# Delta-rule attention turns: each triangular system as two diagonal blocks of 64 and a corner

## The chip, the cores and the metric

The kernel runs on one core of one Trainium2 chip. The core has a matrix engine (PE, with its weight loads listed apart as PEld), a vector engine (DVE), a scalar engine (ACT), a general engine that here mostly issues indirect DMAs (POOL) and a queue for plain DMAs (SP). The metric is device time in microseconds (us) of one execution. Three runs of the kernel before took 1979.56 to 1985.12 us, median 1981.37 us.

## The reference, cut to what matters

Four stages run one after the other on a sequence of 4096 tokens of width 256: a delta-rule attention, a mixture of experts (8 experts, top 2), an RWKV layer and a ternary feed-forward net. The change touches the first only. Its recurrence, cut to the two memories `fH` (fast) and `sH` (slow), is

```
def step(carry, inp):
    pred = (q_t @ fH + q_t @ sH) * 0.5
    d_fast = outer(k_t, v_t) - outer(k_t, k_t @ fH)
    fH = fast_alpha * fH + (1 - fast_alpha) * d_fast
    d_slow = outer(k_t, v_t) - outer(k_t, k_t @ sH)
    sH = slow_alpha * sH + (1 - slow_alpha) * (i_t > 0.5) * d_slow
    ...
    o = p_t[0] * (q_t @ fH) + p_t[1] * (q_t @ sH) + p_t[2] * ns
```

Over a chunk of 128 tokens the steps of one memory are a unit lower triangular system of 128 unknowns, (I + L) Y = X, where L is strictly lower triangular (gram matrix of the keys times decays) and X holds 128 columns: 64 for the values, 64 for the keys.

## The kernel before, in words

The 4096 tokens are 32 chunks of 128. A *turn* (16 of them, `TURNS`) takes two chunks, `j` = 0 and 1, and each chunk has two memories, `m` = 0 and 1, so a turn solves four systems. While the systems of turn t are solved, the same turn carries the *tail* of turn t-1 (state update and outputs, which go from chunk to chunk), the *head* of turn t+1 (transposes, grams, masks, right sides) and, from turn 2 on, one piece per turn of the later work on blocks of 512 tokens (neuron state, output projection, norm, router logits, ranks, places). The pieces for odd turns differ from those for even ones.

Before the change a system is solved by doubling on the right side: Y = (I - L)(I + L^2)(I + L^4)... X, in 8 levels (`LEVELS`), the first 5 of which (`SQUARES`) also square the matrix. `L` holds each matrix and its transpose (128x128 each), because a matmul needs its left operand transposed.

* PE, `level` (L1216): at level n, for each chunk, up to four 128x128 squares into banks 0 and 1 (L1229, L1230), then the product with the two right sides into banks 2 and 3 (L1238). Every fp32 matmul is two PE instructions in the trace.
* ACT, `square` (L968): copies the four squares of a chunk, 128x512, from PSUM to the other buffer of `L` (L972; the last level only the transposes, L975).
* DVE, `apply` (L579): adds the product to the right side `X`, 128x256 a chunk (L588), 16 times a turn. From level 5 on the sums go into `Z` (partial_sums), since no further square is taken: levels 5 to 7 apply the same matrix three times. `masks` (L567) makes `L` from the gram in PSUM: two 128x256 products a chunk (L574) and one for `QM` (L577).

In the trace `X` is part of the tile `st`, and all banks are called `bank`.

Each engine works through a list written out by hand in `turn(u)`, one for PE (L1338), DVE (L751), ACT (L1041) and POOL (L382); semaphores count levels (`sq_ps`, `sq_cp`, `ap_ps`, `ap_rdy`). Nothing is reordered: an engine that waits at level n holds back all that stands behind it in its list. POOL's list also paces the loads of the weight check (`load_words`, L374, which waits for `fold_words` on DVE, L637), adds the hidden weight blocks by DMA in turns 12 to 15 (`hidden_sums`, L399) and scatters the normed tokens to the experts (`scatter`, L345), eight indirect DMAs for each block of 512 tokens. The expert stage starts by gathering from what was scattered (`xg`, L1521), when the last scatter has landed.

Of the kernel before, what the change touches and what calls it, by code (L numbers as in the profile page):

```python
# [25 lines left out]
SQUARES = 5  # L26
# [50 lines left out]
def build(nc, A):  # L77
# [5 lines left out]
    with ctx:  # L83
# [109 lines left out]
        QM = sb("QM", [128, 2, 2, 2, 128], to=pa)  # L193
        YT = sb("YT", [128, 2, 128], to=pa)
# [224 lines left out]
        def _(dve):  # L419
# [146 lines left out]
            dve.sem_inc(pp_rdy, 1)  # L566

            def masks(t, p, j, bk=4):
# [11 lines left out]
            def apply(t, p, n):  # L580
                for j in range(2):

                    dve.wait_ge(ap_ps, t * (2 * LEVELS) + (2 * n + j + 1))
                    if n == 0:
                        dve.wait_ge(x_rdy, t * 2 + (j + 1))
                    x_ = X[:, p, j, :, :, :].rearrange("p a m d -> p (a m d)")
                    z_ = Z[:, j, :, :, :].rearrange("p a m d -> p (a m d)")
                    V.tensor_tensor(z_ if SQUARES <= n < LEVELS - 1 else x_, x_, B[2 + j][:, 0:256],  # L588
                                    ALU.subtract if n == 0 else ALU.add).then_inc(ap_rdy, 1)
# [298 lines left out]
        def _(act):  # L888
# [78 lines left out]
            def square(t, p, n):  # L967
                for j in range(2):  # L968
                    act.wait_ge(sq_ps, t * (2 * SQUARES) + (2 * n + j + 1))
                    src = B[j][:, :].rearrange("p (a n) -> p a n", a=4)  # L970
                    if n < SQUARES - 1:
                        A_.activation(L[:, p, j, (n + 1) % 2, :, :], src, ACT.Copy).then_inc(sq_cp, 1)  # L972
                    else:

                        A_.activation(L[:, p, j, (n + 1) % 2, 1::2, :], src[:, 1::2, :], ACT.Copy).then_inc(sq_cp, 1)  # L975
# [57 lines left out]
            def turn(u):  # L1033
# [34 lines left out]
                at(u, 1, 5, columns, 0)  # L1068
                if head:
# [65 lines left out]
        def _(pe):  # L1135
# [81 lines left out]
            def level(t, p, n, first):  # L1217
                for j in range(2):
                    if n == 0:
                        pe.wait_ge(l_rdy, t * 2 + (j + 1))  # L1220
                        pe.wait_ge(x_rdy, t * 2 + (j + 1))
                    elif n <= SQUARES:
                        pe.wait_ge(sq_cp, t * (2 * SQUARES) + (2 * (n - 1) + j + 1))
                    Ln = L[:, p, j, min(n, SQUARES) % 2, :, :]
                    if n < SQUARES:
                        for m in range(2):
                            a, b_ = Ln[:, 2 * m, :], Ln[:, 2 * m + 1, :]
# [4 lines left out]
                    if n > 0:  # L1232
                        pe.wait_ge(ap_rdy, t * (2 * LEVELS) + (2 * (n - 1) + j + 1))
                    elif not first:
                        pe.wait_ge(ap_rdy, t * (2 * LEVELS) + (j - 1))
                    for m in range(2):
                        right = X[:, p, j, :, m, :] if n <= SQUARES else Z[:, j, :, m, :]
                        last = T.matmul(B[2 + j][:, 0:256].rearrange("p (a m d) -> p a m d", a=2, m=2)[:, :, m, :],  # L1238
                                        Ln[:, 2 * m + 1, :], right, start=True, stop=True)
# [98 lines left out]
            def turn(u):  # L1338

                t, p, deltas, head, tail = u, u % 2, u < TURNS, u + 1 < TURNS, 1 <= u <= TURNS  # L1340
                for n in range(LEVELS):
                    if deltas:
                        level(t, p, n, not tail)
# [2163 lines left out]
```

## Time and profile before

| what | value |
|---|---|
| median of 3 runs | 1981.37 us |
| the profiled execution | 1982.84 us |
| its span, first to last instruction | 1981.0 us |
| PE busy over the span | 1830.8 us (92%) |
| DVE busy | 1468.3 us (74%) |
| ACT busy | 1113.4 us (56%) |
| POOL busy | 307.7 us (16%) |
| the turns | about 89 to 461 us |
| first matmul of the expert stage | 525.3 us |

Busy time is the time in which at least one instruction of an engine runs. A row of the view by windows gives, for a stretch of the span, the busy time of each engine with its number of instructions, the TensorE clock granted (1.00 is full), the share of the DMA engines and what they moved. A turn is taken here from the first transposes of its tail (L1246) to those of the next. In rows of groups, of lines and of the timeline an arrow `out<-in` names the tiles, and brackets give the idle time ahead of an instruction and what ended it. A PE row says which part of the array the matmul uses, rows by columns: `64*128` is a contraction over 64 partitions.

### The profile page before, as it was taken

Reading aid. Unit: us, or ns where it says so; the run is one execution under the profiler, and the core shown is the slowest. Engines: PE = TensorE matmul, PEld = TensorE weight load, DVE = VectorE, ACT = ScalarE, POOL = GpSimd, SP = SyncE. Lnnn points to the kernel's source line nnn. Section 1 sums busy time; section 2 is a strip of 40 time slices with the busy share of each in tenths; the row PEclk is TensorE's granted clock in tenths of the full one; section 3 lists DMA queues with packets and bytes.
Section 4 is the critical chain, followed back from the end, with each engine's and each line's share of the span. In section 5 each row is a group of like instructions: output and inputs, shape, how many; then the busy total and the mean of one; then the engine's idle time right before and its main releaser. Section 6 shows DMA issues by size and latency. Waiting matters only on the chain. (4 is left out here: it accounts for less than half of the span.)

```text
span 1981.0 us, 31299 instructions
## 1 busy us (share of the span) xinstructions
PE 1830.8 (92%) x10880; PEld 1564.9 (79%) x10880; DVE 1468.3 (74%) x2959; ACT 1113.4 (56%) x1997; POOL 307.7 (16%) x282
## 2 busy tenths in 40 slices
PE   7999999997399999999687969999999999999999
PEld 5688888886399999999465647776788888888887
DVE  7567888887477766767689988787776776776675
ACT  3656666664244444343599876664565465466454
POOL 0000002235433223233101011111000000000000
PEclk9999999996699999999799979999999999999999
DMA  3099543359435334322444572333333243142241
GB/s 112 29 378 407 180 161 124 103 117 223 148 65 120 86 86 96 64 44 39 117 106 88 126 210 87 149 117 118 117 139 128 67 167 128 64 170 106 65 170 65
DMA packets 107985, 251.78 MB, mean 127 GB/s; under 512 B 8992, under 2 KB 51616, under 8 KB 99616
## 3 DMA queue, kind: packets, MB, share of 16 engines
q1 hardware_dynamic: 82288, 201.16, 28.6%
q0 software_dynamic: 23680, 46.28, 12.8%
q10 hardware_dynamic: 1888, 2.67, 0.4%
q8 instruction: 75, 1.23, 0.2%
q14 instruction: 54, 0.44, 0.1%
HBM read 172.88 MB, written 107.61 MB: 142 GB/s over the span
## 5 line engine op out<-in xcount | busy, mean ns | idle before, releaser
L1566 POOL DMA_INDIRECT tokens_behind_spare_rows<-yg,row_of_token x70 | 120.2, 1717 | 300.1 <-DVE row_of_token L1729 272.4
L1661 ACT ACTIVATE h<-bank,b1s 128x256 f32<-128x256 f32 x280 | 125.3, 472 | 37.7 <-PE bank L1489 23.4
L1650 ACT ACTIVATE yg<-yt,own_gates 128x256 f32<-128x256 f32 x68 | 31.0, 502 | 191.1 <-DVE yt L1724 184.7
L3244 ACT ACTIVATE hidden_quarter<-hidden_quarter,scl 128x512 f32<-128x512 f32 x96 | 67.6, 721 | 118.9 <-DVE hidden_quarter L3080 118.3
L1238 PE MATMUL bank<-st,L 128*128 128x128 f32 x768 | 117.1, 279 | 13.3 <-DVE st L588 13.2
L972 ACT ACTIVATE L<-bank 128x512 f32<-128x512 f32 x128 | 75.1, 593 | 93.8 <-PE bank L1230 93.5
L2465 PE MATMUL bank<-split_0h,hidden_weights 128*128 128x512 f32 x320 | 126.5, 395 | 0.0
L2465 PE MATMUL bank<-split_1h,hidden_weights 128*128 128x512 f32 x320 | 125.4, 392 | 0.1
L2466 PE MATMUL bank<-split_0l,hidden_weights 128*128 128x512 f32 x320 | 125.3, 391 | 0.0
L2466 PE MATMUL bank<-split_1l,hidden_weights 128*128 128x512 f32 x320 | 125.3, 391 | 0.0
L1230 PE MATMUL bank<-L 128*128 128x128 f32 x640 | 119.0, 276 | 0.0
L1238 PEld LDWEIGHTS bank<-st,L 128*128 128x128 f32 x768 | 100.4, 193 | 17.8 <-DVE st L588 7.0
L588 DVE TENSOR_TENSOR st<-st,bank 128x256 f32<-128x256 f32 x192 | 75.1, 417 | 52.3 <-PE bank L1238 51.5
L1229 PE MATMUL bank<-L 128*128 128x128 f32 x512 | 100.9, 279 | 0.7
L2465 PE MATMUL bank<-split_2h,hidden_weights 128*128 128x512 f32 x256 | 101.4, 396 | 0.0
L1758 DVE TENSOR_TENSOR hsl<-h,hsh 128x512 fp32r<-128x512 f32 x140 | 96.9, 692 | 4.8
L2466 PE MATMUL bank<-split_2l,hidden_weights 128*128 128x512 f32 x256 | 100.2, 391 | 0.0
L1230 PEld LDWEIGHTS bank<-L 128*128 128x128 f32 x640 | 95.1, 193 | 0.0
L3032 DVE SCALAR_TENSOR_TENSOR hidden_quarter<-bank,scl,x_tok 128x512 f32<-128x512 f32 x64 | 47.4, 747 | 55.7 <-ACT x_tok L3207 55.7
L3039 DVE TENSOR_TENSOR split_2l<-hidden_quarter,split_2h 128x1024 fp32r<-128x1024 f32 x48 | 59.1, 1251 | 35.4 <-ACT split_2h L3226 35.4
L1229 PEld LDWEIGHTS bank<-L 128*128 128x128 f32 x512 | 78.8, 193 | 7.2 <-issue 2.7
L1712 DVE COPY raw_gates<-xg 128x8 f32<-128x8 f32 x36 | 8.0, 223 | 102.0 <-PE bank L1594 101.3
(493 smaller groups left out, 6088.3 us busy)
## 6 DMA issues: line engine op xcount, KB each, us to landing
hidden_weights<-hidden_weight_blocks SPq DMA_DIRECT2D x64, 1024.0 KB, 4.8
z_by_expert<-zero SPq DMA_DIRECT2D x64, 520.0 KB, 15.9
hidden_weight_blocks<-in_ffn_dram SPq DMA_DIRECT2D x14, 1024.0 KB, 13.2
ckb<-in_ffn_dram POOLq DMA_DIRECT2D x32, 352.0 KB, 5.5
xg<-z_by_expert SPq DMA_DIRECT2D x36, 260.0 KB, 3.4
x_tok<-in_w_dram SPq DMA_DIRECT2D x8, 1024.0 KB, 7.9
x_tok<-x_T SPq DMA_DIRECT2D x16, 512.0 KB, 6.0
x_tok<-after_time_mix SPq DMA_DIRECT2D x15, 512.0 KB, 8.2
```

What stands on the lines that cost most here:

```text
L588: V.tensor_tensor(z_ if SQUARES <= n < LEVELS - 1 else x_, x_, B[2 + j][:, 0:256], ALU.subtract if n == 0 else ALU.add).then_inc(ap_rdy, 1)
L972: A_.activation(L[:, p, j, (n + 1) % 2, :, :], src, ACT.Copy).then_inc(sq_cp, 1)
L1229: T.matmul(B[j][:, 256 * m:256 * m + 128], b_, a, start=True, stop=True)
L1230: last = T.matmul(B[j][:, 256 * m + 128:256 * m + 256], a, b_, start=True, stop=True)
L1238: last = T.matmul(B[2 + j][:, 0:256].rearrange("p (a m d) -> p a m d", a=2, m=2)[:, :, m, :], Ln[:, 2 * m + 1, :], right, start=True, stop ...
L1566: pool.indirect_dma_start(x2_d, bass.IndirectOffsetOnAxis(to_row[:, j:j + 1].bitcast(u32), 0), yg[:, j, :], None, compute_op=ALU.add).then ...
L1661: nc.scalar.activation(h32[:, m, :], B[m % 4][:, 0:TT], ACT.Gelu_apprx_tanh, bias=b1s[:, e * KH + m:e * KH + m + 1]).then_inc(h_act, 1)
L1758: V.tensor_tensor(hs[1][:, m:m + 2, :], h32[:, m:m + 2, :], f32(hs[0][:, m:m + 2, :]), ALU.subtract).then_inc(h_rdy, 1)
L2465: nc.tensor.matmul(out, w, x[0], start=first, stop=False, **more)
L2466: return nc.tensor.matmul(out, w, x[1], start=False, stop=last, **more)
L3039: V.tensor_tensor(lo[:, ks, :], QB[source_of(use)][:, ks, :], f32(hi[:, ks, :]), ALU.subtract).then_inc(ring_rdy, 1)
L3244: A_.activation(QB[to][:, m, :], src, ACT.Gelu, scale=scl[:, off[lay.name] + row:off[lay.name] + row + 1]).then_inc(g_act, 1)
```

## The change

Each 128x128 system is cut into two diagonal blocks of 64 and the corner below: with L = [[A, 0], [C, B]], the solution is Y1 = (I+A)^-1 X1 and Y2 = (I+B)^-1 (X2 - C Y1). Block A lies on partitions 0 to 63 and block B on partitions 64 to 127 of the same columns (`half`), so that one instruction of DVE or ACT handles both, and PE gets two matmuls, one for each half.

* The inverse is doubled in place of the right side: `apply` 0 sets it to I minus the block (transposed), levels 1 to 5 add the product with the next square, 128x128 a chunk. `twin` is a pair of identities of 64 in what was part of `Z`.
* Squares are 64x64 (two halves, two memories, matrix and transpose), and `square` copies 128x256 a chunk, in the last level 128x128. The copy of square 1 also waits for `apply` 0 of its chunk.
* Level 6 multiplies the corner by the inverse of B (only rows 64 to 127 of the array, output on partitions 0 to 63) and then both inverses by the right sides; `apply` 6 is a copy of 128x256. Level 7 takes the corner's part off on partitions 64 to 127.
* ACT gets `corner_products` (L995), two copies of 64x128, between the columns of the router input and the two `right_side` calls of the next turn. It waits for level 6 on PE.
* `masks` makes the two blocks with two products of 64 partitions and the corner with a third.

A turn has 128 matmuls for its systems where it had 68. Of the 128, 112 have a moving side of 64 columns and 16 one of 128; all stand in blocks of 64x64 of the array.

```diff
-                for m in range(2):
-                    gm = B[bk][:, m * 128:(m + 1) * 128].rearrange("p (o n) -> p o n", o=1)
-                    V.tensor_tensor(L[:, p, j, 0, 2 * m:2 * m + 2, :], gm.broadcast_to([128, 2, 128]),
-                                    maskL[:, m, :, :], ALU.mult)
+                gram = B[bk][:, 0:256].rearrange("p (m o n) -> p m o n", m=2, o=1)
+                for h in range(2):
+                    V.tensor_tensor(pair(p, j, 0)[half[h]], gram[half[h], :, :, half[h]].broadcast_to([DS, 2, 2, DS]),
+                                    maskL[half[h], :, :, half[h]], ALU.mult)
+                V.tensor_tensor(corner(p, j)[half[1]], gram[half[1], :, 0, half[0]], maskL[half[1], :, 0, half[0]], ALU.mult)
...
             def apply(t, p, n):
                 for j in range(2):
-                    dve.wait_ge(ap_ps, t * (2 * LEVELS) + (2 * n + j + 1))
...
-                    V.tensor_tensor(z_ if SQUARES <= n < LEVELS - 1 else x_, x_, B[2 + j][:, 0:256],
-                                    ALU.subtract if n == 0 else ALU.add).then_inc(ap_rdy, 1)
+                    if n == 0:
+                        dve.wait_ge(l_rdy, t * 2 + (j + 1))
+                        V.tensor_tensor(inv, twin, pair(p, j, 0)[:, :, 1, :], ALU.subtract).then_inc(ap_rdy, 1)
+                        continue
+                    dve.wait_ge(ap_ps, t * (2 * (LEVELS - 1)) + (2 * (n - 1) + j + 1))
+                    if n <= SQUARES:
+                        V.tensor_tensor(inv, inv, B[2 + j][:, 0:128].rearrange("p (m n) -> p m n", m=2),
+                                        ALU.add).then_inc(ap_rdy, 1)
+                    elif n < LEVELS - 1:
+                        V.tensor_copy(x_, B[2 + j][:, 0:256]).then_inc(ap_rdy, 1)
+                    else:
+                        V.tensor_tensor(x_[half[1]], x_[half[1]], B[2 + j][half[1], 0:256], ALU.subtract).then_inc(ap_rdy, 1)
...
             def square(t, p, n):
                 for j in range(2):
+                    if n == 1:
+                        act.wait_ge(ap_rdy, t * (2 * LEVELS) + (j + 1))
+                    src = B[j][:, 0:256].rearrange("p (m f n) -> p m f n", m=2, f=2)
...
+            def corner_products(t, p):
+                for j in range(2):
+                    act.wait_ge(sq_ps, t * (2 * SQUARES + 2) + (2 * SQUARES + j + 1))
+                    A_.activation(corner_inverse(p, j)[half[0]], B[j][half[0], 0:128].rearrange("p (m n) -> p m n", m=2),
+                                  ACT.Copy).then_inc(sq_cp, 1)
...
                 at(u, 1, 5, columns, 0)
+                if deltas:
+                    corner_products(t, p)
                 if head:
                     right_side(t + 1, 1 - p, 0)
...
                             if n < SQUARES - 1:
-                                T.matmul(B[j][:, 256 * m:256 * m + 128], b_, a, start=True, stop=True)
-                            last = T.matmul(B[j][:, 256 * m + 128:256 * m + 256], a, b_, start=True, stop=True)
+                                for h in half:
+                                    T.matmul(B[j][h, 128 * m + 64:128 * m + 128], ab[h, m, 0, :], ab[h, m, 1, :], start=True, stop=True)
+                            for h in half:
+                                last = T.matmul(B[j][h, 128 * m:128 * m + 64], ab[h, m, 1, :], ab[h, m, 0, :], start=True, stop=True)
...
+                    if n <= SQUARES:
+                        for m in range(2):
+                            for h in half:
+                                last = T.matmul(B[2 + j][h, 64 * m:64 * m + 64], ab[h, m, 0, :], inv[h, m, :], start=True, stop=True)
+                    elif n < LEVELS - 1:
+                        for m in range(2):
+                            last = T.matmul(B[j][half[0], 64 * m:64 * m + 64], corner(p, j)[half[1], m, :], inv[half[1], m, :],
+                                            start=True, stop=True)
+                        last.then_inc(sq_ps, 1)
+                        pe.wait_ge(x_rdy, t * 2 + (j + 1))
+                        for m in range(2):
+                            for h in half:
+                                last = T.matmul(out[h, :, m, :], inv[h, m, :], X[h, p, j, :, m, :], start=True, stop=True)
+                    else:
+                        for m in range(2):
+                            last = T.matmul(out[half[1], :, m, :], corner_inverse(p, j)[half[0], m, :], X[half[0], p, j, :, m, :],
+                                            start=True, stop=True)
                     last.then_inc(ap_ps, 1)
```

On PE, at level 1 of an odd turn, this is what stands for one chunk and the tail's first matmul behind the second, before the change (L1229 and L1230 are the squares, L1238 the products with the right sides; one row is one matmul unless it says x2):

```order
L1229 MATMUL bank<-L 128x128 [waits square_taken]
L1230 MATMUL bank<-L 128x128
L1229 MATMUL bank<-L 128x128
L1230 MATMUL bank<-L 128x128
L1238 MATMUL bank<-st,L 128x2x64 [waits X_ready]
L1238 MATMUL bank<-st,L 128x2x64
L1256 MATMUL bank<-state,YT 128x128 [waits pred_taken,state_ready,YT_ready]
```

and this is what stands there now (L1257 and L1259 squares, L1267 products with the inverse, each row pair once for the lower and once for the upper half):

```order
L1257 MATMUL bank<-L 64x64 [waits square_taken]
L1257 MATMUL bank<-L 64x64
L1259 MATMUL bank<-L 64x64 x2
L1257 MATMUL bank<-L 64x64 x2
L1259 MATMUL bank<-L 64x64 x2
L1267 MATMUL bank<-L 64x64 [waits X_ready]
L1267 MATMUL bank<-L 64x64 x3
L1297 MATMUL bank<-state,YT 128x128 [waits pred_taken,state_ready,YT_ready]
```

The six matmuls of a chunk became twelve of a quarter of the array each, and the waits stand where they stood.

On ACT, behind the last squares of an odd turn, this stood before the change (L975 the last square, L963 to L965 the head's transposed keys, L1026 the router columns, from L952 on the right sides of the next turn):

```order
L975 ACTIVATE L<-bank 128x2x128 [waits square_in_psum] x2
L963 ACTIVATE st<-bank 128x2x128 [waits decayed_q_ready,kqT_in_psum]
L964 ACTIVATE gram_right_sides<-bank 64x2x128
L965 ACTIVATE gram_right_sides<-bank 64x128
L1026 ACTIVATE zT<-bank 128x512 [waits z1T_in_psum]
L952 ACTIVATE KR<-st,rev 128x64 [waits kq_ready,pred_in_psum]
```

and this stands there now (L993 the last square, L998 the corner products):

```order
L993 ACTIVATE L<-bank 128x2x64 [waits square_in_psum] x2
L979 ACTIVATE st<-bank 128x2x128 [waits decayed_q_ready,kqT_in_psum]
L980 ACTIVATE gram_right_sides<-bank 64x2x128
L981 ACTIVATE gram_right_sides<-bank 64x128
L1050 ACTIVATE zT<-bank 128x512 [waits z1T_in_psum]
L998 ACTIVATE L<-bank 64x128 [waits square_in_psum] x2
L968 ACTIVATE KR<-st,rev 128x64 [waits kq_ready,pred_in_psum]
```

ACT has a new wait, for level 6 of the same turn on PE, ahead of the right sides and all that stands behind them.

## Rows read from the trace of the kernel before

**Rows 1.** Windows, turns 0, 1, 3, 9, 10: us, busy (x) by engine, PEclk, DMA

```profile
89.10:116.67 27.57, 24.13 (x179) 21.98 (x179) 18.88 (x60) 18.62 (x52) 2.15 (x4) 0.94 0.71 260
116.67:136.49 19.82, 19.60 (x168) 18.86 (x167) 13.07 (x41) 12.08 (x36) 1.04 (x2) 1.00 1.03 407
156.31:178.73 22.42, 21.20 (x177) 19.69 (x176) 16.73 (x51) 14.69 (x44) 2.07 (x4) 1.00 1.03 407
295.85:319.70 23.85, 22.64 (x188) 21.03 (x187) 20.08 (x70) 18.80 (x52) 6.03 (x8) 1.00 0.58 188
319.70:343.53 23.83, 22.83 (x195) 21.45 (x194) 18.93 (x68) 12.48 (x36) 6.72 (x8) 1.00 0.24 75
```

**Rows 2.** Lines by form, PE, turns 9 and 10 (295.85 to 343.53 us)

```profile
L1238 PE MATMUL bank<-st,L 128*128 128x128 f32 x98 | 14.9, 278 | 1.6 <-DVE st L588 1.6
L1230 PE MATMUL bank<-L 128*128 128x128 f32 x80 | 14.8, 275 | 0.0
```

**Rows 3.** Waits, turns 9 and 10: total us, times, longest us

```profile
ACT L L972 <- PE bank L1230: 11.6, 10, 3.5
DVE st L588 <- PE bank L1238: 4.8, 5, 1.5
```

**Rows 4.** Timeline, PE, one level of turn 9: start, us, form, count

```profile
307.38 0.39 PE L1230 MATMUL bank<-L 128*128 128x128 f32 x2
...
307.60 0.61 PE L1238 MATMUL bank<-st,L 128*128 128x128 f32 x4
...
308.05 0.61 PE L1230 MATMUL bank<-L 128*128 128x128 f32 x4
```

**Rows 5.** Timeline, PE, matmuls over 64 partitions and their neighbours

```profile
88.09 1.12 PE L1200 MATMUL bank<-vgT,small_weights 64*128 64x512 f32 x2
...
185.86 0.81 PE L1214 MATMUL bank<-gram_right_sides,st 128*128 128x384 f32 x2
186.60 1.14 PE L1308 MATMUL bank<-woN,big 64*128 64x256 f32 x8
187.67 0.49 PE L1229 MATMUL bank<-L 128*128 128x128 f32 x2
```

**Rows 6.** Lines L1160 and L1200: weight loads of 64 and 128 columns, ns min/median/max

```profile
L1160 PEld LDWEIGHTS bank<-hT,small_weights x16: 132/134/136, 26.3 to 95.0; 128*64 128x64 f32 x16
...
L1200 PEld LDWEIGHTS bank<-vgT,small_weights x16: 182/184/186, 23.5 to 88.2; 64*128 64x128 f32 x16
```

**Rows 7.** Lines by form, DVE, turns 9 and 10

```profile
L588 DVE TENSOR_TENSOR st<-st,bank 128x256 f32<-128x256 f32 x24 | 9.2, 416 | 4.9 <-PE bank L1238 4.8
...
L574 DVE TENSOR_TENSOR L<-bank,maskL 128x256 f32<-128x256 f32 x8 | 3.0, 417 | 0.4 <-PE bank L1214 0.4
...
L595 DVE TENSOR_TENSOR Wb<-st,bank 128x128 f32<-128x128 f32 x4 | 1.1, 280 | 0.0
```

**Rows 8.** Lines by form, ACT, turns 9 and 10

```profile
L972 ACT ACTIVATE L<-bank 128x512 f32<-128x512 f32 x16 | 9.4, 593 | 11.6 <-PE bank L1230 11.6
...
L975 ACT ACTIVATE L<-bank 128x256 f32<-128x256 f32 x4 | 1.3, 373 | 0.0
```

**Rows 9.** Timeline behind turn 14: POOL's last check load and scatters, DVE's last places

```profile
439.51 0.58 POOL L374 DMA_DIRECT2D ckb<-in_ffn_dram  x1 [12.15 <-DVE lowb L637]
...
477.48 1.04 POOL L345 DMA_INDIRECT z_by_expert<-Z,slotz  x1 [0.30 <-issue]
...
503.17 0.17 DVE L748 CAST slotz<-SF 128x8 int32<-128x8 f32 x1
...
518.58 0.97 POOL L345 DMA_INDIRECT z_by_expert<-Z,slotz  x1 [0.30 <-issue]
```

**Rows 10.** Windows and PE timeline where the clock fell, turn 0

```profile
109.90:112.90 3.00, 0.20 (x2) 0.00 (x1) 2.69 (x17) 1.54 (x5) 0.00 (x0) 1.00 1.01 408
113.00:116.00 3.00, 2.63 (x12) 2.63 (x13) 1.97 (x4) 0.00 (x0) 1.02 (x2) 0.50 1.03 413
...
114.39 0.64 PE L1229 MATMUL bank<-L 128*128 128x128 f32 x2
```

More of the change, by code:

```diff
@@ L193, in build @@
         QM = sb("QM", [128, 2, 2, 2, 128], to=pa)
+        Lp = L[:, :, :, :, :, :].rearrange("p b j s a n -> p b j s (a n)")
+        pair = lambda p, j, s_: Lp[:, p, j, s_, 0:256].rearrange("p (m f n) -> p m f n", m=2, f=2)
+        inverse = lambda p, j: Lp[:, p, j, 0, 256:384].rearrange("p (m n) -> p m n", m=2)
+        corner = lambda p, j: Lp[:, p, j, 0, 384:512].rearrange("p (m n) -> p m n", m=2)
+        corner_inverse = lambda p, j: Lp[:, p, j, 1, 256:384].rearrange("p (m n) -> p m n", m=2)
+        twin = Z[:, 1, 0, :, :]
         YT = sb("YT", [128, 2, 128], to=pa)
@@ L566, in _ @@
             dve.sem_inc(pp_rdy, 1)
+            for h in range(2):
+                for m in range(2):
+                    go(V.tensor_copy(twin[half[h], m, :], ident[half[h], half[h]]))
             def masks(t, p, j, bk=4):
@@ L1215, in grams, with level @@
                          start=True, stop=True).then_inc(g_ps, 1)
-            def level(t, p, n, first):
+            def level(t, p, n):
                 for j in range(2):
@@ L1225, in level @@
+                    ab, inv = pair(p, j, n % 2), inverse(p, j)
+                    out = B[2 + j][:, 0:256].rearrange("p (a m d) -> p a m d", a=2, m=2)
                     if n < SQUARES:
                         for m in range(2):
-                            a, b_ = Ln[:, 2 * m, :], Ln[:, 2 * m + 1, :]
                             if n < SQUARES - 1:
-                                T.matmul(B[j][:, 256 * m:256 * m + 128], b_, a, start=True, stop=True)
-                            last = T.matmul(B[j][:, 256 * m + 128:256 * m + 256], a, b_, start=True, stop=True)
+                                for h in half:
+                                    T.matmul(B[j][h, 128 * m + 64:128 * m + 128], ab[h, m, 0, :], ab[h, m, 1, :], start=True, stop=True)
+                            for h in half:
+                                last = T.matmul(B[j][h, 128 * m:128 * m + 64], ab[h, m, 1, :], ab[h, m, 0, :], start=True, stop=True)
@@ L1231, in level @@
                         last.then_inc(sq_ps, 1)
[L1232 to L1239, printed above, removed]
+                    if n == 0:
+                        continue
@@ new lines, in level @@
+                    pe.wait_ge(ap_rdy, t * (2 * LEVELS) + (2 * (n - 1) + j + 1))
+                    if n <= SQUARES:
[12 more added lines that the diff above has]
+                    else:
+                        for m in range(2):
+                            last = T.matmul(out[half[1], :, m, :], corner_inverse(p, j)[half[0], m, :], X[half[0], p, j, :, m, :],
+                                            start=True, stop=True)
@@ L1342, in turn @@
                     if deltas:
-                        level(t, p, n, not tail)
+                        level(t, p, n)
                     if tail:
```

20 lines of the change are left out of this document (10 added, 10 removed).

## The prediction

> **What bounds the kernel now.** I first cut the attention stage into turns with the view by windows. From turn 5 to turn 14 a turn lasts 23.85 us, and PE is busy for 22.64 to 22.83 us of it at full clock; DVE is busy for 20.08 us in an odd turn and 18.93 us in an even one, ACT for 18.80 and 12.48 us [rows 1]. Turns 1 and 2 last 19.82 us each with PE at 19.60, turns 3 and 4 some 22.4 us with PE at 21.2, turn 0 27.57 us with PE at 24.13 [rows 1]. So PE is the bound of every turn. The view of waits says the same from the other side: in two turns ACT waits 11.6 us for squares and DVE 4.8 us for products [rows 3]. The lines by form name what fills PE: the squares and the products of the four systems [rows 2], 68 matmuls or 136 instructions a turn.
>
> A saving in the turns must also get through to the end. The timeline behind the turns shows that the expert stage waits for POOL's scatters, not for DVE: the last places are made at 503.17 us, but the last scatter is issued at 518.58 us [rows 9]. POOL's list runs from its last check load at 439.51 us (released by DVE at the end of turn 14) through hidden sums to 32 scatters in one row from 477.48 us on [rows 9]. This chain of some 80 us hangs on the end of turn 14 alone. What turns 0 to 14 save is passed on in full; what turn 15 saves is not, as long as DVE's end stays ahead of POOL's (15.4 us of slack).
>
> **PE's share of the change.** A matmul of 128 columns costs two instructions at 0.112 us: four of L1238 fill the 0.45 us from 307.60 to 308.05 [rows 4]. So the systems now take 136 x 0.112 = 15.2 us a turn, and all else on PE 22.7 - 15.2 = 7.5 us.
>
> The trace has no matmul in a 64x64 block, so its price must be bounded. *Length:* a weight load of 64 columns is 50 ns shorter than one of 128 (134 against 184) [rows 6], and 0.112 less 0.050 is 0.06; half of 0.112 is 0.056. I take 0.058 us an instruction with 64 columns. From above the bound is the full 0.112. *Side by side:* L1308 is four matmuls over 64 partitions, two on the lower half and then two on the upper. Its eight instructions of 256 columns start at 186.60 and are followed at 187.67 [rows 5]. One after the other they would need 8 x 2 x 0.112 = 1.79 us; they took 1.07. A single one over 64 partitions gains nothing: L1200, two instructions of 512 columns, takes 1.12 us, 2 x 4 x 0.112 and its tail [rows 5]. So the two halves ran beside each other, even with the second half two matmuls further down the list. The new code puts the halves next to each other.
>
> The sum a turn, in pairs: 36 pairs of squares and 20 pairs of products, two instructions each at 0.058, make 6.5 us; 4 corner matmuls alone 0.46; 4 pairs of 128 columns at 0.112 make 0.9 and the 4 single ones of level 7 another 0.9. Together 8.8 us. If the halves take turns it is 72 + 40 matmuls at 2 x 0.058 = 13.0, plus 0.46 + 1.8 + 0.9: 16.1 us.
>
> Going in and out of the half-array work costs something: behind L1308 the next pair takes 0.49 us where an undisturbed one takes 0.39 [rows 4, 5], and L1308's 1.07 us are 0.17 over four paired steps of 2 x 0.112. I charge 0.25 us a round trip (0 to 0.3) and count seven a turn, one for each level that has full-array work behind it: 1.75 us. The Trainium skill ("TensorEngine Tiling (Array Packing)", Key Properties) says that a change of tiling mode drains TensorE; the 0.10 us behind L1308 agrees with that, and without the drains the sum would be 1.75 us a turn shorter on PE. PE then needs 7.5 + 8.8 + 1.75 = 18 us of a steady turn, and is no longer the bound.
>
> **What is late next.** DVE. A 128x128 product with PSUM takes 0.280 us, a 128x256 one 0.416 [rows 7]; 12 of the 16 `apply` steps shrink that way, 12 x 0.136 = 1.6 us. The copy of level 6 and the 64-partition step of level 7 keep 256 columns and are charged as before, since an instruction's length follows its columns. The two L574 of a chunk stay at 256 columns, and the corner adds one of 128: 2 x 0.2 = 0.4 us back. Net 1.2 us, so DVE needs 18.9 us in an odd turn and 17.7 in an even one, 18.3 on average. It now waits 23.84 - 19.5 = 4.3 us a turn. If all waiting went, a turn would be 18.3 us; if none went, 22.6. Most of it is for products and squares on PE [rows 3], which come in half the time, but not all can go: after each `apply` DVE needs a matmul, the drain of that matmul and a semaphore back before the next one, and in some levels it has little else to do meanwhile. In odd turns it also waits for ACT.
>
> ACT saves 8 copies from 0.593 to 0.373 us [rows 8], 1.8 us, and pays two corner copies of half a L975's columns, estimated at 0.25: in odd turns 18.8 - 1.3 = 17.5 us. It gets a new wait: behind `corner_products` stand the right sides, the last columns, `prepare`, and then square 0 of the next turn: work that used to fill ACT's idle time behind the squares and now starts only at level 6. With 17.5 us of its own and a wait in the middle, ACT is the second bound of odd turns. I put two thirds of DVE's old waiting on top of its work: 18.3 + 2.9 = 21.2 us.
>
> **The sum.** Turns 5 to 14: 10 x (23.84 - 21.2) = 26.4 us. Turns 1 and 2 have DVE at 13.1 us and PE then at 15: I take 16.5, halfway between PE's work and the old length, 2 x 3.3 = 6.6. Turns 3 and 4: PE 21.2 - 15.2 + 10.5 = 16.5; I take 19.2, 2 x 3.2 = 6.4. Turn 0: PE falls by 4.7 us, but it already waits for DVE at the end [rows 10], so 3.5. Together 43 us. The profiled execution took 1982.84 us (span 1981.0 and 1.84 around it), 1.5 us over the median of the runs, less than they differ by; 1982.8 - 43 = 1940 us.
>
> **Rivals.**
> *A, the forecast*, 1940 us; with turns of 20.2 to 22.6 us its own range is 1915 to 1965.
>
> *B, waits nearly vanish.* If DVE becomes full, a steady turn is 19 us and saves 4.85, the early ones 4 to 5: 10 x 4.85 + 5 x 4.2 = 70, so 1913 us. For it: PE would have 18 us of work and ACT 17.5. Against: three lists in fixed order, each near full, wait for each other.
>
> *C, the halves take turns: slower.* In the 64x64 blocks both halves write the same PSUM bank, while L1308 wrote one bank with each half, so the row does not show this case. PE would need 7.5 + 16.1 + 1.75 = 25.4 us, with its 1 us of waits 26.4, 2.5 over now: 15 x 2.5 = 38, so 2020 us (1997 without the drains). It decides from the point where the systems cost more than 23.85 - 7.5 - 1.75 - 1 = 13.6 us on PE, which is when less than about a third of the 7.3 us between both sums is gained by overlap. For it speaks a rule of the Trainium skill ("TensorEngine Tiling (Array Packing)", Gotcha 1: PSUM Pressure): different row tiles cannot use one PSUM bank at the same time. No run so far shows that. Against: the halves end on different partitions, which L1308's did not. If each small instruction kept 0.112 us and no pair overlapped, it would be 256 x 0.112 = 28.7 us, 13.5 over now, 2185 us; the shorter weight load [rows 6] speaks against that.
>
> *D, the clock falls: slower or nothing.* Before it fell to half at 112.9 us PE had run 0.20 us of 3.0, and at half clock a pair of squares took 0.64 us instead of 0.39 [rows 4, 10]. After the change PE has more gaps. If half of PE's 18 us of work were done at the lower clock, they would be 27, and a turn at least as long: 15 x 3 = 45 over now, 2028 us. Against: that fall came when PE had next to nothing for 3 us at a stretch, while the 3.2 us that a turn would leave it are spread over eight levels.
>
> *E, nothing passes.* DVE keeps all its waits and ACT's new one adds to them: a steady turn of 23.5 and early ones 0.5 shorter, 6 us, 1977 us.
>
> **Chances.** A 0.58, B 0.13, C 0.13, D 0.08, E 0.08. A measurement of this kernel tells about 0.3%, 6 us, from no change. A and B are faster; of E and D a little falls on that side too: faster 0.74. Within 0.3%: half of E and a part of C without drains, 0.08. Slower: 0.18. The range is 1908 to 2000 us: it leaves out the better half of B and most of C and D, nearly 0.2 in all.
>
> **What would show it.** Right: MATMUL rows of the new square lines in pairs with an interval of some 0.06 us, steady turns near 21 us, DVE at 18 to 19 us of each, PE at 1.00, the scatters unchanged in number and still the last to end before the expert stage, which starts some 43 us earlier; from there on all as before. Wrong in the price: rows of the two halves one after the other (C), or a PEclk below 1.00 in the turns (D). Wrong in what is late next: DVE idle as long as before and ACT standing at the corner products, or places on DVE later than the scatters. A change behind 530 us other than the shift would speak against the whole account.

## The result: 1966.0 us, a third of the forecast saving

The changed kernel takes 1965.99 us (median of 6 runs, 1962.74 to 1973.05) beside 1980.46 us of the kernel before (6 runs, 1977.98 to 1985.12). The ratio is 0.9925, with a 95% interval of 0.991 to 0.9941: faster by 0.75%, about 15 us, where 43 were forecast. The profiled execution of after took 1962.74 us with a span of 1961.0.

**The turns after the change.** The view by windows, cut at the first matmul of L1287 (the y transposes, which open a tail), for turns 3, 6, 7, 8, 10, 12 and 14. Columns: the stretch; its length and PE's busy time with its count; then PEld, DVE, ACT, POOL; the granted clock, DMA share, GB/s.

```profile
148.06:172.21 24.15, 21.11 (x294) 17.01 (x295) 16.79 (x53) 13.42 (x48) 2.06 (x4) 0.75 1.03 406
...
214.07:235.44 21.37, 17.98 (x313) 14.79 (x313) 18.80 (x71) 11.61 (x41) 2.06 (x4) 1.00 0.58 197
235.44:257.21 21.77, 17.62 (x306) 14.37 (x307) 19.28 (x71) 16.21 (x51) 2.05 (x4) 1.00 0.68 233
257.21:281.10 23.89, 20.80 (x312) 17.43 (x313) 19.05 (x71) 11.71 (x41) 2.05 (x4) 0.86 0.30 92
...
303.07:326.90 23.83, 20.81 (x313) 16.91 (x313) 18.73 (x71) 11.60 (x41) 6.41 (x8) 0.86 0.25 77
...
349.71:375.19 25.48, 22.38 (x312) 18.45 (x313) 18.67 (x71) 11.72 (x41) 6.44 (x8) 0.80 0.30 93
...
396.80:421.99 25.19, 22.41 (x312) 18.35 (x313) 18.30 (x71) 11.61 (x41) 10.86 (x12) 0.80 0.72 156
```

Read the clock beside the length. Turns 6 and 7, at 1.00, last 21.37 and 21.77 us with PE at 18.0 and 17.6: forecast were 21.2 and 18. The turns at 0.86 last 23.8 to 23.9, as long as any turn before [rows 1]; at 0.80 they last 25.2 to 25.5, longer than before. Before, every turn from 1 on was at 1.00 ([rows 1] has turns 1, 3, 9 and 10).

**The price of the new matmuls.** The timeline of PE in a level of turn 6 (start, us, form, count), the answer to [rows 4]:

```profile
217.46 0.28 PE L1257 MATMUL bank<-L 64*64 64x64 f32 x4
217.58 0.28 PE L1259 MATMUL bank<-L 64*64 64x64 f32 x4
217.70 0.28 PE L1257 MATMUL bank<-L 64*64 64x64 f32 x4
217.81 0.28 PE L1259 MATMUL bank<-L 64*64 64x64 f32 x4
217.93 0.40 PE L1267 MATMUL bank<-L 64*64 64x64 f32 x8
218.26 0.49 PE L1297 MATMUL bank<-state,YT 128*128 128x128 f32 x2
218.68 0.33 PE L1257 MATMUL bank<-L 64*64 64x64 f32 x4
```

Each group of four instructions is two matmuls, one on each half, into one bank. The next group starts 0.117 us later: two steps of 0.058 us. One after the other, four would take 0.23. The last two rows show the way out of the half-array work and back: the eight L1267 fill 0.23 us by that step, and L1297 starts 0.10 us after that; it needs 0.22 us, and the next L1257 starts 0.20 us after that. (A turn's systems have 116 matmuls with 64 columns and 12 with 128, not 112 and 16: the four corner matmuls, L1270, have 64.)

**What PE did before the clock fell.** Its timeline at level 5 of turn 10, and then the windows ahead of the fall and in it:

```profile
314.50 0.49 PE L1297 MATMUL bank<-state,YT 128*128 128x128 f32 x2
315.53 0.41 PE L1235 MATMUL bank<-ident,st 128*128 128x128 f32 x2 [0.54 <-DVE QM L587]
317.03 1.12 PE L1267 MATMUL bank<-L 64*64 64x64 f32 x16 [1.09 <-DVE L L600]
```

```profile
315.00:317.00 2.00, 0.41 (x2) 0.20 (x3) 1.97 (x8) 1.62 (x7) 0.00 (x0) 0.99 0.00 0
317.00:323.80 6.80, 6.77 (x51) 5.05 (x52) 3.00 (x11) 2.75 (x12) 0.00 (x0) 0.50 0.25 80
```

PE waits 0.54 us, works 0.41, waits 1.09. From 317.0 on it is granted 0.50, its lower level of 1.2 GHz, for 6.8 us, in which it is busy without a break while DVE works 3.00 us. But the same waits stand at level 5 of turn 6, which has 1.00 from end to end:

```profile
227.04 0.41 PE L1235 MATMUL bank<-ident,st 128*128 128x128 f32 x2 [0.54 <-DVE QM L587]
228.54 0.65 PE L1267 MATMUL bank<-L 64*64 64x64 f32 x15 [1.08 <-DVE L L600]
```

And before the change a wait of 1.00 us on DVE (L588) stood in each even turn from 4 to 14, with no fall. So a fall follows some of these waits and not others; what decides is not shown by any run here. Nine of the turns 2 to 14 of after show a clock under 1.00, with no wait in these turns over 1.14 us (the fall of turn 1 follows one of 3.5 us at the end of turn 0); over turns 1 to 14 the clock is 0.90, where before had 1.00.

The waits of turn 10 are for DVE, whose list ahead of them reads:

```profile
313.89 0.85 DVE L583 TENSOR_TENSOR L<-bank,maskL 64x256 f32<-64x256 f32 x2
314.66 0.29 DVE L585 TENSOR_TENSOR L<-bank,maskL 64x128 f32<-64x128 f32 x1
314.96 0.42 DVE L587 TENSOR_TENSOR QM<-bank,maskQ 128x256 f32<-128x256 f32 x1
...
315.81 0.87 DVE L696 SCALAR_TENSOR_TENSOR x_tok<-bank,small,x_tok 128x256 f32<-128x256 f32 x2
316.60 0.48 DVE L600 TENSOR_TENSOR L<-L,bank 128x128 f32<-128x128 f32 x2
```

The masks and a residual (L696) stand between PE's products and the L600 that takes them. Another wait of 0.98 us stands at the start of most turns, for L632.

**DVE and ACT.** Lines by form in turns 6 and 7 (an even and an odd one), the two L596 of turn 6 and of turn 7 from the timeline, and a wait, the answers to [rows 7], [rows 8] and [rows 3]:

```profile
L600 DVE TENSOR_TENSOR L<-L,bank 128x128 f32<-128x128 f32 x20 | 5.0, 282 | 1.5 <-PE bank L1267 1.4
L583 DVE TENSOR_TENSOR L<-bank,maskL 64x256 f32<-64x256 f32 x8 | 3.4, 420 | 0.9 <-PE bank L1240 0.8
...
L596 DVE TENSOR_TENSOR L<-partial_sums,L 128x128 f32<-128x128 f32 x4 | 1.5, 425 | 0.0
...
L585 DVE TENSOR_TENSOR L<-bank,maskL 64x128 f32<-64x128 f32 x4 | 1.1, 286 | 0.0
...
L991 ACT ACTIVATE L<-bank 128x256 f32<-128x256 f32 x16 | 5.8, 376 | 7.7 <-PE bank L1259 7.7
```

```profile
215.68 1.06 DVE L596 TENSOR_TENSOR L<-partial_sums,L 128x128 f32<-128x128 f32 x2
238.97 0.49 DVE L596 TENSOR_TENSOR L<-partial_sums,L 128x128 f32<-128x128 f32 x2
```

```profile
ACT L L998 <- PE bank L1270: 4.8, 2, 2.5
```

The mean of 425 ns for L596 is a mixture: 0.28 us each in turn 7, as long as L600, and 0.56 to 0.57 in turn 6. Over the whole trace its median is 284 ns; it is long in turns 3, 4, 6 and 8 alone.

**Behind the turns.** POOL's last check load, its last scatter, DVE's last places and the expert stage's first matmul, the answer to [rows 9]:

```profile
423.45 0.58 POOL L380 DMA_DIRECT2D ckb<-in_ffn_dram  x1 [13.06 <-DVE lowb L653]
...
501.35 0.97 POOL L351 DMA_INDIRECT z_by_expert<-Z,slotz  x1 [0.30 <-issue]
...
487.09 0.17 DVE L764 CAST slotz<-SF 128x8 int32<-128x8 f32 x1
...
508.32 1.12 PE L1635 MATMUL bank<-ident,xg 128*128 128x128 f32 x4 [21.46 <-DMA xg<-z_by_expert]
```

Turn 14 ends 16.9 us earlier (421.99 for 438.88), the last scatter 17.2 and the expert stage's first matmul 17.0 (525.34 before). The chain on POOL carried the saving through unchanged.

### The profile page after: what moved, and what is told of

Its sections match the earlier page's. It is cut to its first block and busy times, and to the rows that moved or that the text cites. A ratio compares the mean times of both kernels' runs of the same rounds, so it can differ in the third digit from the quotient of the medians.

```text
span 1961.0 us, 35208 instructions
## 1 busy us (share of the span) xinstructions
PE 1775.7 (91%) x12800; PEld 1478.8 (75%) x12800; DVE 1459.8 (74%) x2995; ACT 1086.2 (55%) x2029; POOL 306.9 (16%) x282
## 5 line engine op out<-in xcount | busy, mean ns | idle before, releaser
L1259 PE MATMUL bank<-L 64*64 64x64 f32 x1280 | 87.0, 232 | 0.2 <-issue 0.2
L991 ACT ACTIVATE L<-bank 128x256 f32<-128x256 f32 x128 | 46.5, 377 | 70.0 <-PE bank L1259 69.0
L1257 PE MATMUL bank<-L 64*64 64x64 f32 x1024 | 78.0, 243 | 5.8 <-DVE QM L587 5.6
L1528 PE MATMUL bank<-xTh,w_1h 128*128 128x256 f32 x288 | 80.8, 281 | 2.7 <-ACT h L1702 2.7
L1528 PE MATMUL bank<-w_1h,hsh 128*128 128x256 f32 x288 | 82.1, 285 | 0.6 <-DVE yt L1765 0.6
L1529 PE MATMUL bank<-w_1l,hsh 128*128 128x256 f32 x288 | 80.3, 279 | 0.0
L1530 PE MATMUL bank<-w_1h,hsl 128*128 128x256 f32 x288 | 80.3, 279 | 0.0
L1529 PE MATMUL bank<-xTl,w_1h 128*128 128x256 f32 x288 | 80.2, 278 | 0.0
```

The source lines that it names most:

```text
L1257: T.matmul(B[j][h, 128 * m + 64:128 * m + 128], ab[h, m, 0, :], ab[h, m, 1, :], start=True, stop=True)
L1259: last = T.matmul(B[j][h, 128 * m:128 * m + 64], ab[h, m, 1, :], ab[h, m, 0, :], start=True, stop=True)
L1528: nc.tensor.matmul(out, a[0], b[0], start=first, stop=False)
L1529: nc.tensor.matmul(out, a[0], b[1], start=False, stop=False)
L1530: return nc.tensor.matmul(out, a[1], b[0], start=False, stop=last)
```

## The experiments

T1: falls of TensorE's clock inside the turns ate most of the missing gain. T2: ACT's new wait at the corner products sets the turn. T3: DVE's list sets it. Every kernel was timed beside the kernel before on its chip; ratios are to that kernel. The first four ran together (before: 1983.05 us), the next four (1981.61), then the last three (1982.86).

| run | us | ratio (95%) |
|---|---|---|
| after | 1965.99 | 0.9925 (0.991 to 0.9941) |
| e1_fill | 1949.61 | 0.9833 (0.982 to 0.9845) |
| e1_fill_short | 1977.06 | 0.9965 (0.9946 to 0.9983) |
| e2_corner_dve | 1966.28 | 0.9909 (0.9895 to 0.9924) |
| e3_order | 1954.60 | 0.9859 (0.9842 to 0.9875) |
| e4_both | 1943.09 | 0.9803 (0.9786 to 0.9821) |
| e5_mask_twice | 1957.51 | 0.9883 (0.9866 to 0.99) |
| e6_diag | 1946.75 | 0.9818 (0.9804 to 0.9833) |
| e7_diag_order | 1938.06 | 0.9767 (0.9753 to 0.9782) |
| e8_half_fill | 1934.51 | 0.976 (0.9747 to 0.9774) |
| e9_corner_full | 1942.49 | 0.9793 (0.978 to 0.9807) |
| e10_no_start | 1943.24 | 0.9808 (0.9789 to 0.9827) |

**Work for PE's waits** (e1_fill; e1_fill_short has 1 column in the place of 256):

```diff
+            def fill(k, bk=3):
+                for _ in range(k):
+                    T.matmul(B[bk][:, 256:256 + 256], I_, filler[:, 0:256], start=True, stop=True)
...
+                            pe.wait_ge(ap_rdy, t * (2 * LEVELS))
+                            fill(2)
                             y_transposes(t - 1, 1 - p)
...
+                            if n == 0 and tail and u % 2 == 1:
+                                fill(1)
                             transposes(t + 1, 1 - p, n // 4)
...
                         at(u, 1, 3, neuron_back)
+                        if tail and u % 2 == 0:
+                            pe.wait_ge(sq_cp, t * (2 * SQUARES + 2) + 2 * SQUARES)
+                            fill(2, 1)
```

> Adds to TensorE, in every turn after the first, two matmuls of 256 columns that nobody reads (some 0.45 us each) while it waits at the start of the turn, one more ahead of the keys' transposes in odd turns, and two behind level 4 in even turns. T1 (falls of TensorE's clock inside the turns ate the missing gain): PEclk stays at or near 1.00 from turn 1 to turn 14, even turns come down from 23.8-25.5 to 21.5-22.5 us, and the time to 1946-1956 us, 10 to 20 us under the changed kernel's 1966. T2 (ScalarE's new wait at the corner products sets the turn): the clock may rise, but turns keep their length; 1964-1970 us. T3 (VectorE is the bound, because the masks on partition halves cost more than forecast): the same as T2, with VectorE over 95% busy in the turns that were at full clock already.

> The same added matmuls at the same places with the same waits, but of one column instead of 256. All theories: the time of the changed kernel, 1963-1970 us, with the same falls of the clock to half in the turns. T1 stands only if this one does not gain while the long ones do; if both gain, it is the added waits and not the clock.

Turns 9 and 10 with the long fillers, then two turns with the short ones, by windows:

```profile
278.28:299.89 21.61, 19.00 (x313) 15.41 (x313) 19.11 (x71) 16.20 (x51) 6.02 (x8) 1.00 0.61 206
299.89:320.76 20.87, 19.59 (x322) 16.15 (x321) 18.72 (x71) 11.61 (x40) 6.41 (x8) 1.00 0.27 87
```

```profile
288.23:312.11 23.88, 20.76 (x313) 17.47 (x313) 19.29 (x71) 16.20 (x51) 6.03 (x8) 0.86 0.50 164
312.11:336.02 23.91, 21.85 (x320) 18.38 (x321) 18.81 (x71) 11.70 (x41) 6.42 (x8) 0.86 0.23 76
```

PE was given work that nobody reads, and the even turn became 3 us shorter: 20.87 for 23.83. The clock stays at 1.00 from turn 4 to turn 14; the waits for DVE that are left there are 0.9 us at most. That the filler works through the clock alone is seen in turn 6, which is at 1.00 in all three kernels: it lasts 21.37 us in after and 21.36 with either filler. The ratio falls by 0.0092, 18 us, as T1 said. The same places and waits with one column gain nothing; they lose 8 us (1977 where 1963 to 1970 were expected), because now nearly every turn has a fall. That the control is slower than after, and not equal, was in no theory; why the falls come more often there is left open. The difference between the two kernels, 27 us, is that between filler of 256 columns and of 1.

**ACT's wait taken away** (e2_corner_dve): the corner copies move into DVE's level 6.

```diff
-            def corner_products(t, p):
...
                     elif n < LEVELS - 1:
+                        V.tensor_copy(corner_inverse(p, j)[half[0]],
+                                      B[j][half[0], 0:128].rearrange("p (m n) -> p m n", m=2)).then_inc(sq_cp, 1)
                         V.tensor_copy(x_, B[2 + j][:, 0:256]).then_inc(ap_rdy, 1)
```

> The two copies of the corner products go from ScalarE to VectorE (in the list just ahead of the level 6 copy), so ScalarE no longer waits there. T2 (that wait sets the turn): ScalarE's 6.7 us of waiting in turns 9 and 10 go, the right sides and the preparation of the next turn come up to 3.9 us earlier, odd turns shrink by 1 to 3 us; 1942-1955 us. T1 and T3: VectorE gets two copies of 128 columns a turn, about 0.25 us each, on its own path: turns 0 to 0.5 us longer, 1966-1974 us.

The time is that of after. Turns 6 and 7, at full clock as in after, keep their length to 0.05 us:

```profile
214.00:235.37 21.37, 17.86 (x313) 14.80 (x313) 19.09 (x73) 9.93 (x32) 2.06 (x4) 1.00 0.57 193
235.37:257.19 21.82, 17.70 (x306) 14.49 (x307) 19.65 (x73) 17.69 (x54) 2.05 (x4) 1.00 0.68 230
```

In turn 7 ACT no longer waits at that place and DVE works 0.4 us more (19.65 for 19.28), and the turn is as long as it was: ACT's wait is slack, and T2 falls.

**DVE's list in another order** (e3_order): no operation more or less.

```diff
-                at(u, 0, 4, residual, 0)
                 at(u, 1, 3, neurons)
...
                     rows_w(t - 1, 1 - p, 1)
+                at(u, 0, 4, residual, 0)
                 at(u, 0, 4, residual, 1)
...
+                if tail and head:
+                    partial_outputs(t - 1, 1)
                 if head:
                     masks(t + 1, 1 - p, 1)
...
                 if tail and head:
-                    partial_outputs(t - 1, 1)
                     rest_of_outputs(t - 1, 1)
```

> Only VectorE's list is put in another order: the residual of the even turns goes from ahead of level 4's subtraction to behind the last rows of the turn, and the second partial output from behind the masks of the second chunk to ahead of them. T1: TensorE's waits of about 1 us ahead of level 5 and at the turn's start shrink to under 0.5 us, most of the falls of the clock at these two places go, even turns come down by 1 to 3 us; 1945-1960 us. T2: nothing, 1963-1969 us. T3: VectorE has the same work and no fewer microseconds, 1963-1969 us.

The wait of 1.09 us ahead of level 5 became 0.30, and the even turn without a fall is the shortest of all; the turn after it still has one:

```profile
310.48 0.68 PE L1268 MATMUL bank<-L 64*64 64x64 f32 x16 [0.30 <-DVE L L600]
```

```profile
296.71:317.15 20.44, 17.96 (x312) 14.70 (x312) 18.82 (x71) 12.78 (x45) 6.43 (x8) 1.00 0.29 89
317.15:339.67 22.52, 19.10 (x306) 15.72 (x307) 19.29 (x71) 15.04 (x47) 6.05 (x8) 0.92 0.19 58
```

Within T1's interval (1945 to 1960), and it needs no filler: the place of DVE's side work in its list had opened this wait. It is not the cause of all falls. Nine of the turns 2 to 14 still show a lower clock; over turns 1 to 14 it is 0.93, between 0.90 in after and 0.99 with the long fillers. And a part of the gain is not the clock: at 1.00 in both kernels, turn 6 lasts 21.02 us for 21.37 and turn 13 21.24 for 21.61.

**Both together** (e4_both): e1_fill and e3_order, and

```diff
+                            if u == 1:
+                                pe.wait_ge(pp_rdy, 1)
+                                fill(7, 6)
...
+                        if tail and deltas and u % 2 == 1:
+                            pe.wait_ge(sq_cp, t * (2 * SQUARES + 2) + 2 * SQUARES)
+                            fill(2, 1)
                         at(u, 1, 3, neuron_back)
```

> The long fillers of the first experiment, VectorE's list in the order of the fourth, and fillers at the three places where a fall was left: seven ahead of the wait of 3.5 us at the end of turn 0, and two ahead of the neurons' back transposes in odd turns. T1 (the clock): turns 1 and 3 lose another 1 to 1.7 us, every turn from 1 to 14 is at 1.00; with the clock full, the order itself is worth little, since VectorE has the same work: 1943-1950 us beside 1950 for the fillers alone. If the order also shortens waits by itself (the chain through VectorE sets the turn at full clock): 1935-1943 us. If the fillers now stand where TensorE does not wait and delay it: 1950-1957 us.

1943.1 us, where T1's interval ends and that of the shorter chain begins, so the time alone does not choose. All turns from 1 to 14 are at 1.00, turn 3 lasts 19.75 us in place of 24.15; the steady ones 20.9 to 21.4. At full clock the order, with two more fillers in odd turns, is worth 0.4 us in these (21.23 for 21.61) and next to nothing in even ones.

**What sets the turn at full clock?** Four kernels. e5_mask_twice adds to e1_fill one mask operation a chunk; e6_diag changes e1_fill so that one mask operation does for two, at the price of more matmuls. The edit of e5, then that of e6 on DVE and on PE:

```diff
+                V.tensor_tensor(corner(p, j)[half[0]], gram[half[0], :, 0, half[1]], maskL[half[0], :, 0, half[1]], ALU.mult)
```

```diff
-                gram = B[bk][:, 0:256].rearrange("p (m o n) -> p m o n", m=2, o=1)
-                for h in range(2):
-                    V.tensor_tensor(pair(p, j, 0)[half[h]], gram[half[h], :, :, half[h]].broadcast_to([DS, 2, 2, DS]),
-                                    maskL[half[h], :, :, half[h]], ALU.mult)
...
+                gram = B[bk][:, 0:256].rearrange("p (a m o n) -> p a m o n", a=2, m=2, o=1)
+                V.tensor_tensor(pair(p, j, 0), gram[:, 0].broadcast_to([128, 2, 2, DS]), maskL[:, :, :, half[0]], ALU.mult)
...
-                T.matmul(B[bk][:, 0:384], KQT[:, p, j, 0, :], GR[:, j, :, :].rearrange("p a n -> p (a n)"),
+                for h in half:
+                    T.matmul(B[bk][h, 0:128], KQT[:, p, j, 0, h], GR[:, j, 0:2, h], start=True, stop=True)
+                T.matmul(B[bk][half[1], 128:256], KQT[:, p, j, 0, half[1]], GR[:, j, 0:2, half[0]], start=True, stop=True)
+                T.matmul(B[bk][:, 256:384], KQT[:, p, j, 0, :], GR[:, j, 2, :], start=True, stop=True).then_inc(g_ps, 1)
```

> The kernel with the long fillers, and a second mask operation of the corner's size for each chunk (on the other half of the partitions; nothing reads it), 0.29 us twice a turn on VectorE. T3 at full clock (VectorE's list sets the turn once the clock is kept): turns 0.4 to 0.6 us longer, 15 turns, 1955.5-1959 us beside the fillers' 1950. If VectorE's waits absorb it: 1949-1952 us.

> The kernel with the long fillers, with TensorE writing the two diagonal blocks of each Gram matrix side by side (four matmuls in the place of one, the same 384 columns), so that one mask operation of 128x256 takes the place of the two on partition halves: VectorE 0.42 us less a chunk, 0.84 us a turn. If VectorE's list sets the turn at full clock: 0.5 to 0.9 us a turn less, 1936-1942 us. If it does not: 1948-1952 us.

Turns 9 and 10 of e5_mask_twice, then of e6_diag, to be read against the 21.61 and 20.87 us of e1_fill:

```profile
279.42:301.56 22.14, 19.01 (x313) 15.42 (x313) 19.58 (x73) 16.41 (x52) 6.04 (x8) 1.00 0.61 202
301.56:322.75 21.19, 19.45 (x321) 16.13 (x321) 19.04 (x73) 11.53 (x39) 6.42 (x8) 1.00 0.27 86
```

```profile
274.37:295.84 21.47, 19.31 (x326) 16.14 (x325) 18.45 (x69) 16.05 (x51) 6.03 (x8) 1.00 0.63 209
295.84:316.85 21.01, 20.37 (x333) 17.01 (x332) 18.05 (x69) 11.70 (x41) 6.42 (x8) 1.00 0.29 87
```

With 0.79 us more on DVE the two turns are 0.85 longer. (The 1957.5 us of e5 lie in the interval for DVE's list, but its profiled execution also has a fall, in turn 11, which lasts 24.76 us; the turns at 1.00 are the evidence.) With 1.33 us less on DVE and 1.09 more on PE the two turns are the same, 42.48 us. The 1946.75 us of e6 lie in neither interval, 1936 to 1942 nor 1948 to 1952: DVE's work counts where it is added, but taking it away at PE's expense gives nothing in these turns.

e7_diag_order joins e4_both and e6_diag; e8_half_fill is e7 with `256:256 + 128` and `filler[:, 0:128]`; e9_corner_full is e7 with the edit of e2; e10_no_start is e7 with `fill(2 if u == 1 else 0)` at the turn's start.

> Everything of the other three together: long fillers at all places, VectorE's new order, diagonal Gram blocks with one mask operation. If VectorE's list sets the turn: the gains add up, 1928-1940 us. If not: 1943-1950 us, as the fillers with the new order.

> The fastest version so far (fillers at all places, VectorE's new order, diagonal Gram blocks; 1938 us) with fillers of 128 columns in the place of 256, so TensorE has about 0.9 us a turn less to do. If TensorE, at 20 of 21 us with the fillers, now sets the turn: 0.3 to 0.9 us a turn less, 1925-1934 us. If the chain from engine to engine sets it: 1936-1940 us. If the shorter fillers no longer keep the clock up: turns with falls of 2 to 2.5 us each, 1945-1965 us.

> The fastest version so far with the two corner copies on VectorE in the place of ScalarE. T2 at full clock (ScalarE's wait at the corner products, 5.0 us in two turns, sets the turn): 0.5 us or more a turn less, 1925-1932 us. If VectorE's list or its chain with TensorE sets it: two copies more, 0.2 to 0.5 us a turn longer, 1941-1946 us. If neither is near the edge: 1936-1940 us.

> The fastest version so far without the two fillers at the start of each turn after the first, where VectorE's new order has already taken most of TensorE's wait away. If these are not needed for the clock and only fill TensorE: clock still at 1.00, 0 to 0.9 us a turn less, 1925-1938 us. If the clock falls without them: turns 2 us longer where it does, 1945-1965 us.

e7 gains (1938.1), as expected if DVE counts, but its steady turns are only 0.3 us shorter than e4's in odd turns and 0.15 longer in even ones: in the profiled executions turns 0 to 14 end 2.0 us earlier than in e4 (394.58 for 396.62), so most of the 5 us between the medians is not found there. e8, with PE's filler halved, has the lowest time here: 1934.5 us, 48 us (2.4%) under before in its group; against e7 its interval overlaps, so it is not shown to be faster than that. It lies between the interval for PE's list (1925 to 1934) and that for the chain (1936 to 1940). PE lost 1.5 us of filler in two turns and these shrank by 0.4, and two turns have a fall again. e9 is 4 us slower than e7; the intervals just touch, but its turns 11 and 12 at 1.00 last 21.22 and 21.19 us for 20.92 and 21.03: ACT's wait is not it at full clock either. e10 is 5 us slower, 1943.2, between its two intervals (1925 to 1938 and 1945 to 1965): without the fillers at the start the clock falls again in turns 6, 8, 11 and 12, which last 22.2 to 24.05 us. In no kernel did a steady turn get under 20.4 us: neither ACT's wait nor the whole of DVE's or PE's list sets it alone. That the chain from engine to engine does is what remains; no run isolates it.

## Why the prediction was wrong, step by step

**The price of the matmuls: right.** 0.058 us an instruction, halves side by side; PE needs 17.6 to 18.0 us of a turn at full clock (forecast 18), so PE stopped being the bound. The way out of the half-array work and back costs 0.30 us in the rows of turn 6, near the 0.25 that was charged. Rival C is refuted by the rows of turn 6. It rested on the Trainium skill ("TensorEngine Tiling (Array Packing)", Gotcha 1: PSUM Pressure), which has different row tiles unable to use one PSUM bank at once; here two halves wrote one bank, and the trace shows them in the time of one.

**What is late next: nearly right in sum, wrong in parts.** A steady turn was to last 21.2 us; at full clock it lasts 21.37 and 21.77, and 20.87 and 21.61 with the fillers. DVE was to fall by 1.2 us a turn; over turns 1 to 14 it fell by 0.4 (252.60 us before, 246.76 after). The term that was mis-sized is the masks: 1.49 us a chunk (313.89 to 315.38) where they took 1.08 (308.58 to 309.66, the rows below), 0.41 more and not 0.2, so 0.4 us a turn above the forecast.

```profile
308.58 0.75 DVE L574 TENSOR_TENSOR L<-bank,maskL 128x256 f32<-128x256 f32 x2
309.25 0.41 DVE L577 TENSOR_TENSOR QM<-bank,maskQ 128x256 f32<-128x256 f32 x1
```

L585 adds 0.29, and an operation that changes the half no longer overlaps the one before: two L583 take 0.85 us at 0.420 each, and L587 starts 0.01 us after L585 ends, while before two L574 of 0.417 [rows 7] took 0.75. L585, on the same half as the L583 ahead of it, still starts 0.08 us before that one ends. The Trainium skill ("VectorE: DVE Perf Modes", Two Vector instructions with no wait between them) gives as a model that an operation whose operands start in another quarter of the partitions than the one before waits until all earlier ones have finished; the rows of L583, L585 and L587 agree. The 12 shorter `apply` steps came as forecast, but for L596 in turns 3, 4, 6 and 8, where the pair takes 1.06 us in place of 0.49 (0.16 us a turn on average); the 0.2 us a turn that is left is not located. ACT was over-feared: 16.2 us in an odd turn for 17.5, and its wait costs nothing (e2, e9).

**The clock: the step that failed.** The sum has every turn at 1.00: a falling clock is in it with nothing. The prediction gave rival D 0.08, with the words that the fall of turn 0 "came when PE had next to nothing for 3 us at a stretch", while the waits of a turn would be spread. The runs showed a lower clock in nine of the turns 2 to 14, with no wait over 1.14 us in them; with the longest waits filled the clock stayed at 1.00 from turn 4 on and the kernel gained 18 us (e1_fill), and with fillers of one column neither came. The Trainium skill ("TensorE: Matmul & The Clock Gate", A second HAM failure mode) tells of a kernel whose PE idles briefly between groups of matmuls and whose clock swings; the trace agrees (waits of 0.54 and 1.09 us, then 0.50 from 317.0 us on), and the prediction should have weighed it. The ledger of what turns 0 to 14 save, in us, from the turns' boundaries in the traces (turn 1 begins at 116.67 before, 112.00 after, 114.50 in e1_fill, 110.38 in e4_both; turn 5 at 200.81, 192.19, 192.54, 185.54; turn 15 at 438.88, 421.99, 405.84, 396.62):

| turns | forecast | after | e1_fill | e4_both |
|---|---|---|---|---|
| 0 | 3.5 | 4.7 | 2.2 | 6.3 |
| 1 to 4 | 13.0 | 4.0 | 6.1 | 9.0 |
| 5 to 14 | 26.4 | 8.3 | 24.8 | 27.0 |
| sum | 42.9 | 16.9 | 33.0 | 42.3 |

In turns 5 to 14 the forecast was right but for the clock: with it kept up, 24.8 of 26.4 us come, over lists that are 1.4 to 1.8 us a turn longer on PE (turns 7 and 6). In turns 1 to 4 a part of the gap is the clock too (turn 3 at 0.75): in e4_both, with the clock at 1.00 and DVE's new order, they save 9.0 of 13.0, turns 3 and 4 lasting 19.75 and 19.31 us, near the forecast's 19.2. The 16.5 us of turns 1 and 2 were too short: turn 2 of after, at 1.00, lasts 17.33 us, and with the fillers of e4_both they last 18.34 and 17.76. That the sum of e4_both meets the forecast's is in part luck: it saves more in turn 0 and less in turns 1 to 4, with another order on DVE. So the truth was the forecast's turn with D's mechanism on top, at 0.4 to 4.6 us in each turn from 5 to 14 that has a fall (after beside e1_fill: turn 9 21.97 and 21.61 us, turn 12 25.48 and 20.86): neither alone.

**Two side sums.** Turns of 20.2 us would save 36.4 + 16.5 us, so 1930 us and not the 1915 of A's own range; and rival C without drains comes to 1995, not 1997. The forecast hangs on neither.

**The way to the end: right.** All that turns 0 to 14 saved reached the expert stage (16.9, 17.2, 17.0 us). From there on the profiled executions of all kernels differ by up to 7 us among themselves (1451.8 to 1459.0 us), so the single profiles (20.1 us apart) and the medians (14.5) need not agree.

## What to carry to other kernels

When an edit takes work from a TensorE that was full, its granted clock is no longer certain: look which waits will open, and price them at the lower level too. Before adding anything, move side work on the engine that TensorE waits for behind the operation that it waits for (13 us by the ratios here, with no operation added); work for TensorE to do in the waits is worth it when the clock would fall (18 us). An operation cut into halves of the partitions costs its columns twice (two L583 of 64x256 take 0.85 us): count instructions and columns, not elements. And a mean over two turns can mix two lengths, as that of L596 does: look at the rows.

## What had not been expected of the hardware

Filler matmuls that lengthen PE's list by 1.4 to 1.8 us a turn shortened turn 10 by 3 us. And matmuls in different corners of the array run into each other in the timeline: the corner products (L1270, 64 columns, one quarter) and the diagonal products behind them in the list (L1276, 128 columns) interleave in e1_fill. No full-array work stands between these two, so the rows say nothing about the drains that the prediction charged:

```profile
315.47 0.33 PE L1276 MATMUL bank<-st,L 64*64 64x128 f32 x2
315.56 0.28 PE L1270 MATMUL bank<-L 64*64 64x64 f32 x2
315.63 0.28 PE L1276 MATMUL bank<-st,L 64*64 64x128 f32 x2
315.68 0.28 PE L1270 MATMUL bank<-L 64*64 64x64 f32 x2
```
